# Corners of a sample: one wide VectorE product per three taps, summed by accumulating fp32 transposes

## What is computed

```python
for yi in (y0, y0 + 1.0):
    for xi in (x0, x0 + 1.0):
        wgt = (1.0 - jnp.abs(y - yi)) * (1.0 - jnp.abs(x - xi))
        ...
        g = jnp.take_along_axis(feat_flat, idx, axis=2).reshape(B, C, *y.shape[1:])
        out = out + g * (wgt * valid)[:, None]
...
sampled = _bilinear_gather(xp, y, xc)
out = jnp.einsum('bckhw,ck->bchw', sampled, dw_w.reshape(C, K * K))
```

## Time and profile before

| | |
|---|---|
| median of 3 runs | 2748.88 us (2744.28 to 2750.78) |
| span of the profiled execution | 2488.4 us |
| what the median has beyond that span | 260.5 us |
| busy shares of the span | PE 76%, DVE 79%, ACT 47%, POOL 45% |
| first layer's gathers | 49 to 464 us |
| second layer's gathers | 928 to 1350 us |

### The profile page before, as it was taken

How to read it: one execution, slowest core, us unless ns; L and a number is a source line. 1 busy time by engine, 2 the same in 40 slices (tenths; PEclk the granted TensorE clock), 3 DMA queues, 4 the chain that set the end, 5 groups by cost and what they waited for, 6 DMA issues and landing times. The chain is left out here.

```text
span 2488.4 us, 47348 instructions
## 1 busy us (share of the span) xinstructions
PE 1895.0 (76%) x11383; PEld 1003.2 (40%) x11383; DVE 1958.8 (79%) x4888; ACT 1176.8 (47%) x2916; POOL 1115.7 (45%) x1423
## 2 busy tenths in 40 slices
PE   4354444579999964444544799999999999999998
PEld 2344444434444433444444333333434343433432
DVE  4777777689999956777676988788888787888882
ACT  2333333321110013333333367777777777777776
POOL 2777777679898846777776400000000000000000
PEclk8667666689999987666666989999999999999999
DMA  7977777300000038777775400000000001010101
GB/s 239 291 205 205 205 205 204 103 1 1 1 0 1 0 105 266 204 206 203 205 204 150 157 13 22 21 26 21 25 22 24 23 18 29 14 27 14 31 2 39
DMA packets 114148, 232.20 MB, mean 93 GB/s; under 512 B 19423, under 2 KB 64528, under 8 KB 113680
## 3 DMA queue, kind: packets, MB, share of 16 engines
q0 software_dynamic: 51840, 169.91, 23.5%
q1 hardware_dynamic: 62096, 59.79, 8.4%
HBM read 195.72 MB, written 31.46 MB: 91 GB/s over the span
## 5 line engine op out<-in xcount | busy, mean ns | idle before, releaser
L1023 DVE TENSOR_REDUCE l_mx<-ps 128x1 f32<-128x384 f32 x1728 | 848.1, 551 | 146.6 <-PE ps L1125 141.5
L962 ACT ACTIVATE l_e<-ps 128x384 f32<-128x384 f32 x1728 | 719.3, 498 | 229.0 <-PE ps L1110 221.9
L202 POOL DMA_INDIRECT l_corner<-table,l_idx_s x648 | 632.8, 977 | 278.9 <-issue 216.9
L1125 PE MATMUL ps<-l_ka,l_qs 96*128 96x384 bf16 x1728 | 578.8, 336 | 28.4 <-POOL l_v_s L885 18.3
L379 DVE SCALAR_TENSOR_TENSOR l_samp<-l_corner,l_wts_s,l_samp 128x128 f32<-128x128 f32 x1944 | 560.2, 348 | 44.1 <-ACT l_samp L292 21.9
L1110 PE MATMUL ps<-l_qs,l_ks 99*128 99x384 bf16 x1728 | 568.8, 333 | 7.1 <-ACT l_e L962 6.5
L292 ACT ACTIVATE l_samp<-l_corner,l_wts_s 128x128 f32<-128x128 f32 x648 | 213.5, 393 | 506.6 <-DMA l_corner<-table,l_idx_s 506.2
L894 POOL CAST l_nsp<-l_nm 128x3 bf16<-128x3 f32 x96 | 18.1, 189 | 907.9 <-DVE l_nm L1027 830.9
L1187 PE MATMUL ps<-l_e,l_v_s 128*32 128x384 f32 x3456 | 372.4, 503 | 0.0
L562 POOL TENSOR_TENSOR l_prod<-l_prod 128x384 f32<-128x384 f32 x324 | 340.1, 1067 | 49.5 <-DVE l_prod L669 36.9
L1125 PEld LDWEIGHTS ps<-l_ka,l_qs 96*128 96x128 bf16 x1728 | 169.5, 98 | 402.1 <-DVE l_mx L1023 299.5
(11 more groups left out here) (137 smaller groups left out, 1316.6 us busy)
## 6 DMA issues: line engine op xcount, KB each, us to landing
table<-l_tok SPq DMA_DIRECT2D x32, 640.0 KB, 7.5
l_corner<-table,l_idx_s POOLq DMA_INDIRECT x648, 3.7
qk_parts<-l_part SPq DMA_DIRECT2D x12, 576.0 KB, 4.4
l_ka<-qk_parts SPq DMA_DIRECT2D x96, 72.0 KB, 2.3
l_ks<-qk_parts SPq DMA_DIRECT2D x96, 72.0 KB, 2.4
l_qs<-qk_parts SPq DMA_DIRECT2D x96, 48.0 KB, 2.0
x_map<-in_x SPq DMA_DIRECT2D x2, 1152.0 KB, 6.4
l_qs<-qk_parts SPq DMA_DIRECT2D x96, 24.0 KB, 1.7
```

The source lines that it names most:

```text
L202: nc.gpsimd.indirect_dma_start(corner[:, slot, k, :], None, table[b], bass.IndirectOffsetOnAxis(ap=idx_s[:, slot, k:k + 1], axis=0),).then ...
L962: nc.scalar.activation(e[:, slot, i, :], ps[:, ST + (kt * CT + i) % RING, 0:QC], ACT.Exp).then_inc(s["exp"], 1)
L1023: nc.vector.tensor_reduce(mx[:, slot, u // NQC, u % NQC:u % NQC + 1], ps[:, AB + u % RING, 0:CH], AX.X, ALU.max).then_inc(s["max"], 1)
L1125: nc.tensor.matmul(ps[:, AB + u % RING, 0:CH], qs[0:KROWS, chunk // CT % BATCHES, q0:q0 + 128], ka[:, chunk // NQC % 2, (u % NQC) * CH:(u ...
```

## The change

The four corners are no longer added by ScalarE and VectorE. VectorE multiplies all four corners of a group's three taps in place by their weights, with one tensor_tensor of 128x1536 for each group (the weights broadcast along the 128 channels, read from `wts` directly). TensorE turns each of the twelve corner blocks with a transpose and lets the four of one tap accumulate on the same place in PSUM, so the sum is made there. ScalarE keeps only the copies of indices and of the turned samples. `samp` and `wts_s` are gone. GpSimd waits, before it gathers a group anew, for TensorE's transposes of that group (`turned_mm`) and no longer for VectorE.

```diff
-                        pool.wait_ge(s["summed"], 3 * GROUPS * i + (3 * gr + 3))
+                        pool.wait_ge(s["turned_mm"], GROUPS * i + (gr + 1))
...
-                def first_corner(turn, slot, last=False):
-                    i = turn * SLOTS + slot
-                    act.wait_ge(s["summed"], 3 * GROUPS * i + 3 * GROUPS)
-                    nc.scalar.copy(wts_s[:, slot, :], wts[:, bass.ds(i * K2 * 4, K2 * 4)]).then_inc(s["weighed"], 1)
...
-                    for gr in range(GROUPS):
-                        act.wait_ge(gather[slot][gr], turn * (16 * GK) + 16 * GK)
-                        for k in range(gr * GK, (gr + 1) * GK):
-                            ins = nc.scalar.activation(samp[:, slot, k, :], corner[:, slot, k, 0:128],
-                                                        ACT.Copy, scale=wts_s[:, slot, 4 * k:4 * k + 1])
-                        ins.then_inc(s["first_corner"], 1)
-                    if not last:
-                        take_indices(i + SLOTS, slot)
+                def next_indices(turn, slot):
+                    act.wait_ge(gather[slot][GROUPS - 1], turn * (16 * GK) + 16 * GK)
+                    take_indices(turn * SLOTS + slot + SLOTS, slot)
...
-                def sum_corners(turn, slot):
+                def weigh(turn, slot):
                     i = turn * SLOTS + slot
                     for gr in range(GROUPS):
-                        dve.wait_ge(s["first_corner"], GROUPS * i + (gr + 1))
-                        for j in range(1, 4):
-                            for k in range(gr * GK, (gr + 1) * GK):
-                                last = nc.vector.scalar_tensor_tensor(
-                                    samp[:, slot, k, :], corner[:, slot, k, j * 128:(j + 1) * 128],
-                                    wts_s[:, slot, 4 * k + j:4 * k + j + 1], samp[:, slot, k, :],
-                                    ALU.mult, ALU.add)
-                            last.then_inc(s["summed"], 1)
-                            if j < 3:
-                                dve.wait_ge(s["summed"], 3 * GROUPS * i + (3 * GROUPS * SLOTS + 3 * gr + j))
+                        dve.wait_ge(gather[slot][gr], turn * (16 * GK) + 16 * GK)
+                        four = corner[:, slot, gr * GK:(gr + 1) * GK, :].rearrange("p k (j c) -> p (k j) c", c=128)
+                        at = wts[:, bass.ds(i * (K2 * 4) + gr * (GK * 4), GK * 4)]
+                        nc.vector.tensor_tensor(four, four, at.unsqueeze(2).to_broadcast([128, GK * 4, 128]),
+                                                ALU.mult).then_inc(s["weighed"], 1)
...
-                        pe.wait_ge(s["summed"], 3 * GROUPS * i + 3 * GROUPS * (SLOTS + 1))
                         pe.wait_ge(s["turned"], i + 1)
-                        for k in range(K2):
-                            last = nc.tensor.transpose(ps[:, 3 * slot + k // 3, (k % 3) * 128:(k % 3 + 1) * 128],
-                                                       samp[:, slot, k, :], g["ident"][:, :])
-                        last.then_inc(s["turned_mm"], 1)
+                        for gr in range(GROUPS):
+                            pe.wait_ge(s["weighed"], GROUPS * i + (gr + 1))
+                            for k in range(GK):
+                                for j in range(4):
+                                    last = nc.tensor.matmul(
+                                        ps[:, 3 * slot + gr, k * 128:(k + 1) * 128],
+                                        corner[:, slot, gr * GK + k, j * 128:(j + 1) * 128], g["ident"][:, :],
+                                        start=(k == 0 and j == 0), stop=(k == GK - 1 and j == 3), is_transpose=True)
+                            last.then_inc(s["turned_mm"], 1)
```

More of the change, by code:

```diff
@@ L141 @@
 SAMPLE_SEMS = GN_SEMS + ("zeroed pw_mm image off_mm offs tok_mm tok ot_mm mask chain index table0 table1 "
-                         "gap gaps copied gather00 gather01 gather02 gather10 gather11 gather12 first_corner "
-                         "weighed summed turned_mm turned out_mm added diag passed")
+                         "gap gaps copied gather00 gather01 gather02 gather10 gather11 gather12 "
+                         "weighed turned_mm turned out_mm added diag passed")
 def sampling_layer(nc, g, modulated):
@@ L169, in sampling_layer @@
         idx_s = sb("idx_s", [128, SLOTS, K2], I32)
-        wts_s = sb("wts_s", [128, SLOTS, K2 * 4])
         corner = sb("corner", [128, SLOTS, K2, 4 * 128])
-        samp = sb("samp", [128, SLOTS, K2, 128])
         turned = sb("turned", [128, SLOTS, K2 * 128])
@@ L281, in _ @@
                 act.wait_ge(s["index"], B)
[L283 to L296 removed]
+                def next_indices(turn, slot):
+                    act.wait_ge(gather[slot][GROUPS - 1], turn * (16 * GK) + 16 * GK)
+                    take_indices(turn * SLOTS + slot + SLOTS, slot)
                 def take_turned(turn, slot):
                     i = turn * SLOTS + slot
[L300 removed]
+                    act.wait_ge(s["turned_mm"], GROUPS * i + GROUPS * (1 + SLOTS))
                     act.wait_ge(s["out_mm"], i + 1)
@@ L303, in take_turned @@
                                    ps[:, 3 * slot:3 * slot + 3, 0:CH]).then_inc(s["turned"], 1)
-                first_corner(0, 0)
+                next_indices(0, 0)
                 with act.Fori(0, TURNS - 1) as turn:
-                    first_corner(turn, 1)
+                    next_indices(turn, 1)
                     take_turned(turn, 0)
-                    first_corner(turn + 1, 0)
+                    next_indices(turn + 1, 0)
                     take_turned(turn, 1)
-                first_corner(TURNS - 1, 1, last=True)
                 take_turned(TURNS - 1, 0)
@@ L316, in _ @@
             def _(dve):
-                dve.sem_inc(s["summed"], 3 * GROUPS * SLOTS)
                 dve.sem_inc(s["added"], SLOTS)
@@ L398, in add @@
                     nc.vector.bn_stats(g["bst"][:, :, :, :].rearrange("p b t e -> p (b t e)")[:, bass.ds(i * 6, 6)], xt)
-                sum_corners(0, 0)
+                weigh(0, 0)
                 with dve.Fori(0, TURNS - 1) as turn:
-                    sum_corners(turn, 1)
+                    weigh(turn, 1)
                     add(turn, 0)
-                    sum_corners(turn + 1, 0)
+                    weigh(turn + 1, 0)
                     add(turn, 1)
-                sum_corners(TURNS - 1, 1)
+                weigh(TURNS - 1, 1)
                 add(TURNS - 1, 0)
@@ L459, in _ @@
                     pe.wait_ge(s["diag"], 1)
-                pe.sem_inc(s["turned_mm"], SLOTS)
+                pe.sem_inc(s["turned_mm"], GROUPS * SLOTS)
                 pe.sem_inc(s["out_mm"], SLOTS)
```

## The result

The changed kernel took 2756.5 us (median of 12 runs), the kernel before 2746.7 us beside it: ratio 1.0035, 95% interval 1.0019 to 1.0052.

What follows compares the result with a forecast made beforehand. GpSimd's gather issue, 11.5 us per tile, was taken as the bound. Holds by long products +176 us, short holds gone -19: 2645 on the 2488.4 us span, plus 260.5 carried over: 2906 us, range 2780 to 2985.

Steps and rivals of the forecast that it cites:

- rival B: Products hold gathers only briefly whatever their length, up to 0.16 us: no change, 2749 to 2753 us; chance 5%.
- (1): VectorE: three products of 1.76 us replace 27 per tile, 5.3 us for 8.1; worth nothing by itself.
- (2): ScalarE loses nine activations and a copy of weights per tile, off the path: nothing gained.
- (3): TensorE: 36 transposes per tile for 9, 4.0 us at 2.4 GHz; its tile some 10 us, hidden.
- rival C: TensorE at 1.2 GHz bounds the tile, 13.1 us for 11.5, if no gather is held: 2838 us; chance 6%.
- (4): GpSimd's wait for free buffers moves from VectorE's product to TensorE's transposes: free at worst some 8 us after landing, hidden.
- (5): Each long VectorE product holds a gather until 1.64 us after its start, about 0.82 us per product: +176 us.
- rival D: Phase locks badly, so every product costs the gathers 1.2 us or more: 2990 us and up; chance 4%.
- (6): The gathers' holds by the old short VectorE products disappear: -19 us over 648 gathers.
- (7): From a layer's last gather start to its last statistics, 14 to 18 us for 15.4: counted 0.
- A: Long products hold no gather, so only the saving from short holds remains: 2729 us; chance 13%.

Runs made afterwards that it cites:

- e1: The kernel before, unchanged, run again with a new profile: 2734.2 us.
- e16: The changed kernel, unchanged, run again: 2755.6 us against 2488.7 us for the kernel before, ratio 1.108.
- e9: The kernel before with GpSimd also writing 250 unread columns after each gather of the second sampling layer: 2686.0 us; the kernel before took 2746.6 us.
- e17: The kernel before with GpSimd also writing 250 unread columns after each gather in both sampling layers, second run: 2647.0 us, ratio 0.963 to the kernel before.
- e3: The changed kernel with each group's product split into twelve of 128x128: 2769.9 us, ratio 1.011 to the kernel before.
- e2: The changed kernel with each group's product split into three of 128x512: 2685.8 us, ratio 0.982 to the kernel before.
- e4: The changed kernel with TensorE's first release of the corner buffers moved to its program's start: 2724.9 us, ratio 1.095 to the kernel before.
- e5: The changed kernel with TensorE's first buffer release at its program's start and products split into three of 128x512: 2538.7 us, ratio 1.021 to the kernel before.
- e18: The kernel before with 54 transposes and 4 increments added to TensorE's program ahead of each sampling layer's loop: 2751.5 us; the kernel before took 2741.5 us.
- e10: The kernel before gathering half of each table row, the other two corners left at zero: 2750.4 us; the kernel before took 2746.6 us.
- e15: The kernel before with GpSimd also writing 250 unread columns after each gather in both sampling layers, first run: 2646.0 us, ratio 1.064 to the kernel before.

## Why the prediction was wrong

Where the spans went, in us, from the gathers' first and last rows:

| stretch | before, quiet (first profile) | before, late (e1) | after, late | after, quiet (e16) |
|---|---|---|---|---|
| start to first gather | 49.2 | 49.9 | 56.0 | 58.0 |
| gathers of the first layer | 415.1 | 529.0 | 523.6 | 525.7 |
| between | 464.1 | 463.7 | 486.6 | 485.5 |
| gathers of the second layer | 421.2 | 543.0 | 523.7 | 521.6 |
| after the last gather | 1138.7 | 1146.8 | 1157.0 | 1154.7 |
| span | 2488.4 | 2732.4 | 2747.0 | 2745.6 |

**The step that failed is the base:** "The median, 2748.9 us, lies 260.5 above that span, and I carry this over." A run's time lies 1.8 to 2.9 us above its own span in every run that has both (2748.8 for 2747.0, 2734.2 for 2732.4). So 260.5 us could not be overhead around the span; nearly all of them lay inside the span of the runs that made the median, in the layers that the change edits: 241 us of pauses that the profiled execution hardly had. The prediction added its steps to a median with these pauses as if they would stay. The changed kernel has next to none in either kind of job (3 and 2 us). Pacing alone does that (e9, e17), and holds of 1.1 us per product are a pace: three of them to nine gathers, 1.62 us from one gather to the next on the mean (523.6 / 324). When most of the hold is taken away, the pauses return: extra 235, 164 and 36 us go with pauses of 3, 86 and 128 us in the changed kernel, e3 and e2, all in late jobs. So in a late job 235 us of holds took the place of 241 us of pauses. That the two sums are nearly the same, and that the result lies within 4 us of rival B's 2749 to 2753 us, is chance: B's hold was 0.1 us, and 1.09 were measured.

Against the quiet base, to which the steps belong, they gave 2488 + 157 = 2645; measured were 2745.6 (e16), 257 more than before. So the base is not the only fault: the steps themselves were 100 us short. One by one, with e16 against the first profile:

- **(1) VectorE's product**: right, 1.76 us.
- **(2), (3) ScalarE, TensorE**: hidden, right. In e16 GpSimd waited for L450 51 times, 17 us in all, of which 15 are the usual 0.3 us between two gathers. 172 of the 216 groups of twelve transposes ran at a granted clock of 0.95 or more, in 1.47 us each on the median, 4.4 us per tile for the 4.0 of step (3). So the full clock of 2.4 GHz came for most transposes, and rival C's 7.7 us per tile did not.
- **(4) GpSimd's wait**: right inside the loop, missed ahead of it. The first release of the buffers was VectorE's at its program's start and is now TensorE's behind `pe.wait_ge(s["index"], B)`: "PEq L440" above. 33 us (8.8 and 23.8). e4 brings both starts back. It doesn't gain all of it: its span is 23 us shorter than e16's, since its second layer's gathers take 9 us more, with the pause of the earlier trace rows back (6.0 us).
- **(5) The hold**: mechanism right, size too small: 236 us for 176, 1.09 us per product for 0.82. I walked the phase; in the trace 99 of 216 products (115 in the changed kernel's first profile) begin 0.1 to 0.4 us ahead of a gather, where the hold is longest. The late phase was rival D's idea (1.2 us), and the truth lies nearer to it than to mine. e5 against e4 shows the length at work: 45 us in pieces of a third, and 186 us less in time.
- **(6) Short holds gone**: 20 us for 19, right.
- **(7) Ends**: counted 0, -9 us (from the last gather's end to the last statistics it is 4.7 and 3.9 us shorter). The 6.5 us pause of the earlier trace rows went too; with e16's own pauses -5.
- **In no step:** the attention, +20 us, and the involution, +2. In the attention TensorE stops at the loop's back edge 6 times, 38.0 us in all for 18.3 in this pair, 36 to 40 in every profile of the changed kernel and its variants and 17 to 19 in every one of the kernel before and its. The page names GpSimd's copy L885 for the 18.3 us, but in the first such stop TensorE goes on 0.8 us after that copy's end, and in the changed kernel 4.0 us after it. The DMA records show what differs. In each stop of the kernel before one set of instruction loads runs (16 KB on queue 8, twice 8 KB on queue 14), landed 1.7 to 2.1 us after TensorE's last matmul. In each stop of the changed kernel's first profile and of e16 a second set follows, begun 3.3 to 4.1 us after that matmul, and TensorE goes on only when it has landed. e18 has one set in each stop. So the 20 us go with a second load in a row; no run shows why this program needs it.

236 - 20 + 33 - 9 - 5 + 22 = 257. *A* and *B* fell by the table of leads, *C* by TensorE's waits: TensorE doesn't bound a tile.

At step (5) the Trainium skill's SBUF — State Buffer, section Who interferes with whom, was weighed. The traces agree with its first half, by which a VectorE instruction with two SBUF inputs contends with a GpSimd one that reads SBUF; that it is the gather's read that waits, no run shows. Its inference that descriptor generation is not stalled by tensor_tensor is contradicted by gathers of 2.5 us, and of 6.6 us in e3.

What stays open is why a job is quiet or late, and by what the gathers' pace makes increments late. The same chip showed both kinds, and so did the same program; no row of a trace tells the cause.

## What to carry to other kernels

- Set a run's time against its own span before using either. A gap of hundreds of microseconds between the span that you read and the median that you forecast is a second behaviour, and it has to be placed before any term is added to it.
- Split long VectorE tensor_tensors of two SBUF inputs beside indirect gathers: pieces of 128x512 cost a fifth of the hold (45 us for 233). Long close rows of pieces can still hold a gather to their end, 33 times in e3 with 128x128, once in e5 with 128x512. Whether room between the pieces helps was not tested. And none of these kernels was faster than the kernel before in a quiet job.
- A token that moves to another engine moves behind all that this engine waits for first: look at its first release too.

## What the runs showed of the hardware

- In late jobs increments by TensorE and VectorE (not ScalarE) took effect up to 13.7 us late while gathers were issued 1.25 us apart; in 32 of the 34 pauses of e1 the engine that waited went on 2.3 to 3.1 us after the last issued gather's end. In quiet jobs VectorE's add, which waits for TensorE, never started over 0.2 us after the matmuls' end. Half the bytes changed nothing (e10), the pace did (e9, e17). The trace of the kernel before holds 30,690 records of semaphore updates in the quiet execution and 21,875 in e1; whether the others were merged or only not recorded, it doesn't tell. Missing records alone make no pause: the paced kernel has 31,344 in e15 and 27,530 in e17, at the same time.
- A gather that begins under a product is held until 0.12 us before the product's end, at lengths of 0.35, 0.69 and 1.76 us. The edge is sharp: gathers begun up to 0.042 us after a product of 128x1536 lost nothing in e16, those begun 0.047 us or more after it the whole 1.6 us. Products 0.202 us apart (e3) or 0.602 us apart at 0.68 us of length (e5) held some gathers to 0.13 us before the row's end and most only for one product; the kernel before's L379, 0.26 us apart within its threes, held none for longer than 0.2 us.
